# Filling a PSUM buffer by an ACT copy in place of PE transposes, in chunks 1 to 4 of a graph attention kernel's first layer

## What is computed

```python
h = x @ W
s, d = h @ a_src, h @ a_dst
e = leaky_relu(s[src] + d[dst], 0.2)
m = segment_max(e, dst)
ex = exp(e - m[dst])
out = segment_sum(ex[:, None] * h[src], dst) / segment_sum(ex, dst) + b
```

## Time and profile before

| | |
|---|---|
| median of 3 runs | 786.67 us (786.62 to 789.50) |
| the profiled execution | 787.33 us |
| its span, first to last instruction | 785.6 us |
| busy: PE, DVE, ACT, POOL | 670.2, 721.2, 509.3, 324.7 us (85, 92, 65, 41%) |
| share of the chain that ended last | DVE 31%, PE 25%, issue 10% |
| granted TensorE clock, mean | 0.939 |
| products L1548 on PE, 3450 records | 411.1 us |
| row transposes L1532 on PE, 75 | 11.6 us |
| DVE's waits for L1532 | 5.0 us in 4 places |

### The profile page before, as it was taken

One profiled execution on the slowest core, in us unless ns is written; L12 is line 12 of the kernel. 1 busy time (PEld: TensorE's weight loads), 2 busy tenths in 40 slices (PEclk: granted clock), 3 DMA queues, 4 the chain that ended last, 5 costly groups with the idle time before them and its releaser, 6 DMA issues.

```text
span 785.6 us, 14032 instructions
## 1 busy us (share of the span) xinstructions
PE 670.2 (85%) x5692; PEld 649.3 (83%) x5692; DVE 721.2 (92%) x947; ACT 509.3 (65%) x778; POOL 324.7 (41%) x293
## 2 busy tenths in 40 slices
PE   4345999889986999999999989989888979898894
PEld 4345888888885989999999979889878969898894
DVE  5499999999967999999999899999999899999994
ACT  0054444444346987878887769888768777687681
POOL 1504000000004544536385537556476746374662
PEclk9997788898786999999999999999999999999998
DMA  3400000000002000000010010000010010010001
GB/s 97 115 0 1 1 1 2 1 1 1 1 7 17 1 18 17 1 18 1 4 22 17 6 20 17 1 17 1 2 11 29 1 24 18 16 33 2 17 2 37
DMA packets 22062, 11.75 MB, mean 15 GB/s; under 512 B 12254, under 2 KB 19916, under 8 KB 21991
## 3 DMA queue, kind: packets, MB, share of 16 engines
q1 hardware_dynamic: 21190, 9.53, 5.5%
q0 software_dynamic: 800, 1.26, 0.7%
HBM read 9.14 MB, written 1.64 MB: 14 GB/s over the span
## 4 chain that ended last, share of the span: by engine, by line
DVE 31%; PE 25%; issue 10%; POOL 1%; DMA 1%; DVEq 0%; ACT 0%; POOLq 0%
PE ps L1548 21%; DVE ps L844 15%; DVE scratch L922 8%; DVE ps L846 2%; PE ps L1601 1%; PE ps L1579 1%; DVE mu L856 1%; DVE scratch L844 1%; DVE e_top L859 1%; DVE bn6c L906 1%; DMA gathered<-ext_lines 1%; DMA ext_lines<-ext 0%; PE ps L1571 0%; PE ps L1518 0%; POOL scratch L579 0%
## 5 line engine op out<-in xcount | busy, mean ns | idle before, releaser
L1548 PE MATMUL ps<-hB,scratch 125*125 125x129 f32 x3450 | 411.1, 277 | 38.9 <-DVE scratch L922 34.6
L1548 PEld LDWEIGHTS ps<-hB,scratch 125*125 125x125 f32 x3450 | 393.9, 189 | 51.7 <-DVE scratch L922 46.3
L579 POOL TENSOR_TENSOR scratch<-scratch 125x625 f32<-125x625 f32 x165 | 229.3, 1395 | 209.3 <-ACT scratch L1319 209.3
L844 DVE SCALAR_TENSOR_TENSOR ps<-C,a_unit,ps 125x625 f32<-125x625 uint8 x330 | 279.4, 864 | 2.1
L922 DVE SCALAR_TENSOR_TENSOR scratch<-ps,r_src,C 125x625 f32<-125x625 f32 x210 | 180.5, 859 | 5.4 <-PE ps L1532 5.0
L1483 PE MATMUL ps<-scratch 128*128 128x125 bf16 x1250 | 148.5, 296 | 25.4 <-DVE scratch L758 19.2
L1483 PEld LDWEIGHTS ps<-scratch 128*128 128x128 bf16 x1250 | 143.0, 121 | 30.0 <-DVE scratch L758 23.5
L1314 ACT ACTIVATE scratch<-gathered,r_inv 125x625 f32<-125x625 f32 x165 | 133.4, 808 | 37.7 <-PE ps L1548 35.5
L1319 ACT ACTIVATE scratch<-scratch,r_src 125x625 f32<-125x625 f32 x165 | 147.8, 896 | 0.0
L1194 ACT ACTIVATE C<-ps 125x1750 uint8<-125x1750 f32 (+3 forms) x50 | 74.1, 1487 | 97.4 <-PE ps L1483 97.4
L1317 ACT ACTIVATE scratch<-C 125x625 f32<-125x625 uint8 x165 | 117.7, 713 | 9.6 <-POOL scratch L579 9.6
(11 more groups left out here) (145 smaller groups left out, 440.3 us busy)
## 6 DMA issues: line engine op xcount, KB each, us to landing
gathered<-g_lines SPq DMA_DIRECT2D x14, 305.2 KB
xr<-in_x SPq DMA_DIRECT2D x1, 1562.5 KB
out<-xr SPq DMA_DIRECT2D x5, 312.5 KB
edge_sb<-in_edges SPq DMA_DIRECT2D x1, 805.7 KB
gathered<-ext_lines SPq DMA_DIRECT2D x5, 122.1 KB
w<-in_W SPq DMA_DIRECT2D x2, 128.0 KB
gathered<-in_edges,start_i POOLq DMA_INDIRECT x5, 6.1
ext_lines<-ext SPq DMA_DIRECT2D x5, 1.0 KB
```

Of the source, the lines that this page charges most:

```text
L579: g.tensor_tensor(A, A, wide[n % 2], ALU.mult).then_inc(pool_done, 1)
L844: v.scalar_tensor_tensor(dest, counts, unit[:, s:s + 1], top, ALU.min, ALU.max).then_inc(S.top_done, 1)
L1548: last = mm(ps[0:P, acc_at(t):acc_at(t) + HW], A[:, P * t:P * (t + 1)], feat, start=opens and t in (0, 3), stop=closes, skip_group_check=True)
```

## The change

A function `rows_by_act(q)` is true for q = 1 to 4. For these, PE leaves `fast_rows(q)` out, with its waits. ACT does `copy_rows(q)` instead, as the last thing in step 24 of chunk q - 1, behind that step's row maximum: it waits until the SBUF copy has been loaded and until DVE's last product of chunk q - 1 is done, copies the 125x625 float32 row from `ga` in SBUF to `ROWU` in PSUM, and counts `rows_ready` up. For chunk 0 and from chunk 5 on everything is as it was.

```diff
+        def rows_by_act(q):
+            return 0 < q < NC
+
@@ scalar engine
+            def copy_rows(q):
+                act.wait_ge(ga_loaded, 16 * q)
+                act.wait_ge(prod_done, prod_no(q, 0))
+                a_.activation(tiles(ROWU), ga[q % 2].rearrange("p (t n) -> p t n", n=P),
+                              ACT.Copy).then_inc(F.rows_ready, 1)
+
@@ scalar engine, chunk(q), behind the loop over row_maximum
+                    if s == T - 1 and rows_by_act(q + 1):
+                        copy_rows(q + 1)
@@ tensor engine, chunk(q)
-                    if s == rows_at(q) and q < Q - 1:
+                    if s == rows_at(q) and q < Q - 1 and not rows_by_act(q + 1):
                         fast_rows(q + 1)
```

## The result

| | before | after |
|---|---|---|
| median of six runs each | 787.36 us (786.49 to 789.50) | 794.79 us (794.00 to 795.89) |
| ratio | | 1.0098, 95% interval 1.0084 to 1.0113 |
| the profiled execution, its span | 787.33, 785.6 us | 795.89, 794.2 us |
| mean granted TensorE clock | 0.939 | 0.939 |

The kernel became 7.4 us slower by the medians (8.6 us between the two profiled executions, of which the changed kernel's is its slowest); 794.3 was forecast. Three groups of the changed kernel's whole span say where the change sits. The products of DVE (L925, the old L922) now wait 11.3 us for ACT's copy in four places, where they waited 5.0 us in four for PE's transposes; of those one is left (1.1 us). The transposes (L1543, the old L1532) are 55 instead of 75; the copy (L1328) takes 702 ns.

The account below looks back on a forecast made before the run. A PE, DVE, PE chain was taken to set each chunk's 34.68 us, DVE being late early on. Boundary delays of 5.91 + 1.74 = 7.65 us gave 794.98, less 0.66 to the median: 794.3 us, range 790.4 to 797.8.

Parts of the forecast that it names:

- The place of the copy on ACT: At four chunk boundaries: copy starts 0.09 us before the row maximum ends, takes 0.70 us, and delays DVE's product 0.
- The forecast's 7.65 us of added waiting: DVE's product 0 starts 1.97 us later at three boundaries (5.91) and 1.74 us later at chunk 0 to 1.
- PE's saving is off the path: At four boundaries PE loses five transposes, 0.56 us of chain, but only reaches the next chunk earlier and waits there.
- PE's pause: PE idle some 1.5 us before each chunk's first product, waiting for DVE's product 0.
- The wait of 0.5 us that was to stay before step 6: PE still idle some 0.5 us before step 6 in the changed kernel, waiting for DVE's step-6 product.
- This comes through whole: Chunk 0 to 1: the 1.74 us delay reaches PE whole, since chunk 1's step-6 product is waited for too.
- Rival C, the clock: PE's pauses lower the granted clock in chunks 1 to 3: 5% of 69 us, 3.5 us more, 797.8 us; chance 0.08.
- A: Stretch to step 6 bound by PE, so only PE's own first-product delay counts: sum 3.8 us, 790.5 us; chance 0.10.
- B: Copy finished by 313.18, so DVE doesn't wait and PE gains 0.56 us at four boundaries: 784.5 us; chance 0.04.
- PE would gain its 0.56 us: At each of four boundaries, if the copy is early, PE saves the transposes' 0.56 us, 2.2 us in all.

Follow-up runs that it names:

- The two last runs: Copy at start of step 23, mu and m_top in PSUM, later step-5 row maximum, against kernel before: 779.79 us; same without ACT's copy: 782.37 us.

## Why the prediction was right, point by point

- **The place of the copy on ACT: right.** The copy starts 0.13 us before the end of the row maximum and takes 0.71 (0.67 at the first boundary; 0.70 was taken). DVE's waits were forecast as about 3.2 us at three boundaries and 1.7 at the first, and are 3.16, 3.27 and 3.27, and 1.65. The forecast's 7.65 us of added waiting measured 7.52. The runs with the copy two places and one place earlier (1.0007, 1.0025) and with two copies (1.0170) show that it is this chain.
- **"PE's saving is off the path": right for this place.** The two last runs price it at 2.6 us where nothing else stands in the way.
- **PE's pause: right** (1.35 us for the forecast's 1.5), and at the first boundary 2.75. The wait of 0.5 us that was to stay before step 6 came before step 4.
- **"This comes through whole": wrong in size, in both directions.** The step was that DVE's later start shifts all behind it alike. It doesn't, because DVE's small instructions depend on where POOL stands. In chunks 2 and 3 e_top no longer met POOL's multiplication and gave 0.5 us back: the period is 36.14, not 36.65. In chunk 4 a_neg met it instead (0.98 us for 0.17) and with it the chunk lost 0.6.
- **Rival C, the clock: it came true at one boundary**, and with it one of the prediction's own signs of being wrong (a granted clock below 1.00 in chunks 1 to 3). It was priced as a mean over three chunks, from a row far away, whose 0.95 is itself a mean: in the kernel before the clock is 0.50 from 675.7 to 679.1, from 709.9 to 713.2, from 744.0 to 747.4 and at the very end, and 1.00 between. What comes is one such stretch of 3.4 us, in the changed kernel in chunk 1 only. Of that chunk's rest of 1.33 us, mu's wait of 0.40 is PE at the lower clock; the rest, 0.83 us of e_top and back and 0.1 at the tops, is seen in DVE's timeline, and what share of it the clock caused is open.
- **Rivals A and B didn't come.** A needed PE to be free of DVE at step 6; before, it was not, and the periods grew by more than 1.2 us. B needed a copy before 313; even then the time was 1.0007 and not lower, so B's price was wrong too: its step "PE would gain its 0.56 us" left out that PE's step 0 hangs on ACT's move of the sums and that DVE's chain to step 6 hangs on POOL.

So the total was right, with the main term right to 0.1 us. The further terms, +1.9 and -1.0 us, were not forecast and leave 0.9: 7.65 forecast, 8.4 in the first layer of the two profiled executions. That the medians differ by 7.4, still nearer to the forecast, is in part luck; by the ratio's interval it could be 6.6 to 8.9.

## What to carry to other kernels

An engine with idle time can still be the wrong place for one more instruction: read what stands ahead of it in that engine's order and on whom that waits. Here the same copy at three places cost nothing that can be told (1.0007), 0.25% and 0.98%. Where a stall lengthens a pause of TensorE, look at the granted clock behind it: here it was 0.50 for 3.4 us behind some pauses of 2 to 3 us and not behind others, and what DVE then waited for PE's slow transposes was between nothing and 0.4 us. And a short instruction on the path whose duration differs from chunk to chunk is a lead: compare its end with the end of what other engines ran beside it.

## What the runs showed of the hardware

**DVE's small instructions were held until POOL's ended.** e_top (two SBUF inputs of 125x5) took 0.15 to 1.17 us before; in the rows above its end lies within 0.02 us of the end of a POOL multiplication each time, at 322.79, 356.85 and 359.66. With mu in PSUM all fifteen took 145 to 166 ns. back and zk, also with two SBUF inputs, were held in turn once the instruction ahead was not. DVE's 210 products, which read one tensor in SBUF and one in PSUM, took 0.82 to 0.87 us, whatever POOL did. The Trainium skill, "SBUF — State Buffer", section "Who interferes with whom", says that a DVE instruction with two SBUF inputs shares a read interface with POOL, that the shared ports are an exclusive lock, and that the order of issue decides who blocks. The trace agrees: DVE, second here, stood for up to 1.17 us. The hold of a_neg, which has one tensor input, is seen in the durations (0.98 and 1.15 us for 0.17) but wasn't tried by itself; the same section counts such a form (tensor_scalar) among those that can take the shared ports, under conditions that were not looked into here.

**The granted clock fell behind some pauses of PE and not behind others**, from 1.00 to 0.50 (from the 2.4 to the 1.2 GHz level) for 3.4 us each time. In chunks 1 to 4 it fell behind 3.37, 2.75, 2.61 and three times 1.96 us, and not behind 2.28, 2.27 and 1.35 us. In the third layer of the kernel before it fell behind pauses of 2.17, 2.11 and 2.17 us (end of the first at 674.34) and not behind one of 2.11 (end at 638.96). So length alone doesn't tell. At the lower level ten records of products took 2.52 us instead of 1.36 and five transposes 1.11 instead of 0.71.

**ACT wrote PSUM as fast as SBUF**: 0.71 us for 625 float32 from SBUF (0.67 at the first boundary), and 0.74 us for the same copy into SBUF (352.07 above).
